# Decay blocks of 64 tokens instead of 128 in a chunked state-space scan, with the x of the states weighed from the transposed x

## What is computed

```python
x = layernorm(h); x = rmsnorm(x, norm_w)
z, xBC, dt_raw = split(x @ in_proj_w)          # 2048, 3072 and 32 columns
xs, B, C = split(silu(conv4(xBC) + conv_b))    # depthwise, 4 taps
dt = softplus(dt_raw + dt_bias); dA = exp(-dt * exp(A_log))
h_t = dA_t * h_{t-1} + (dt_t * x_t) B_t        # the scan over 512 tokens
y_t = h_t C_t + D * x_t
out = (groupnorm(y * silu(z)) * gate_norm_w) @ out_proj_w + residual
```

## Time and profile before

| | |
|---|---|
| median of 3 runs | 1308.03 us (1307.38 to 1315.56) |
| the profiled execution, its own time | 1308.41 us |
| its span in the trace | 1306.5 us |
| busy share: PE, DVE, ACT, POOL | 80%, 84%, 75%, 66% |
| instructions in the trace | 29881 |

### The profile page before, as it was taken

One profiled execution on the slowest core, in us unless ns is written; L12 is line 12 of the kernel. 1 busy time (PEld: TensorE's weight loads), 2 busy tenths in 40 slices (PEclk: granted clock), 3 DMA queues, 4 the chain that ended last, 5 costly groups with the idle time before them and its releaser, 6 DMA issues. The chain is left out here.

```text
span 1306.5 us, 29881 instructions
## 1 busy us (share of the span) xinstructions
PE 1042.0 (80%) x8556; PEld 718.9 (55%) x8556; DVE 1099.3 (84%) x1837; ACT 985.1 (75%) x2943; POOL 863.5 (66%) x584
## 2 busy tenths in 40 slices
PE   1423778888888888888888889979898888887786
PEld 1412555566555555665566566656566655653555
DVE  8756888889888888888888888888888999947995
ACT  3624778989788878888888888888888888862453
POOL 1540367877677868776777777776777888795321
PEclk9986789999899989998998998899988999998899
DMA  5532244534344334343443444443434344421301
GB/s 148 162 84 53 61 104 99 120 98 98 87 122 111 98 91 109 105 99 90 110 109 98 100 103 110 95 109 91 115 93 93 103 123 106 106 75 43 111 26 33
DMA packets 84864, 127.10 MB, mean 97 GB/s; under 512 B 18512, under 2 KB 29392, under 8 KB 84432
## 3 DMA queue, kind: packets, MB, share of 16 engines
q1 hardware_dynamic: 80464, 122.91, 37.4%
q10 hardware_dynamic: 4224, 2.10, 0.5%
HBM read 115.54 MB, written 9.44 MB: 96 GB/s over the span
## 5 line engine op out<-in xcount | busy, mean ns | idle before, releaser
L1047 DVE SCALAR_TENSOR_TENSOR conv<-bank,cw,conv 128x511 f32<-128x511 f32 (+2 forms) x576 | 412.0, 742 | 105.7 <-ACT conv L763 100.9
L619 POOL TENSOR_TENSOR lm<-lm,cbs 128x1024 f32<-128x1024 f32 x128 | 303.3, 2370 | 87.9 <-ACT xw L755 86.5
L1036 DVE TENSOR_TENSOR_SCAN lm<-spread,bank 128x512 f32<-128x512 f32 x256 | 297.5, 1203 | 16.5 <-issue 12.7
L796 ACT ACTIVATE xdt<-bank,dt_all 128x64 f32<-128x64 f32 x1024 | 221.0, 326 | 0.5 <-issue 0.5
L605 POOL TENSOR_TENSOR gated<-gated,gate 128x512 f32<-128x512 f32 x128 | 163.0, 1273 | 64.5 <-DVE gated L1079 62.7
L1347 PE MATMUL bank<-xn_hi,w_hi 128*128 (+1 forms) x320 | 161.1, 503 | 54.1 <-DVE conv L1047 54.1
L755 ACT ACTIVATE xw<-xdt,lm 128x64 f32<-128x64 f32 x768 | 196.2, 338 | 0.0
L625 POOL TENSOR_TENSOR ssum<-ssum,sq 128x512 f32<-128x512 f32 x96 | 123.5, 1287 | 109.8 <-ACT sq L810 107.5
L1408 PEld LDWEIGHTS bank<-lm,xdt 128*64 128x64 f32 x2048 | 112.6, 140 | 96.4 <-issue 95.6
L611 POOL TENSOR_TENSOR gated<-gated,rbs 128x512 f32<-128x512 f32 x128 | 164.1, 1283 | 1.5 <-ACT rbs L859 1.5
L763 ACT ACTIVATE conv<-bank,cb_bias,cw 128x512 f32<-128x512 f32 x192 | 142.2, 767 | 25.3 <-PE bank L1349 25.3
(11 more groups left out here) (167 smaller groups left out, 1676.3 us busy)
## 6 DMA issues: line engine op xcount, KB each, us to landing
spread<-decay_scratch SPq DMA_DIRECT2D x128, 512.0 KB, 5.1
spread<-product_scratch SPq DMA_DIRECT2D x256, 128.0 KB, 5.6
lm<-in_L_attn_in_proj_w SPq DMA_DIRECT2D x1, 2048.0 KB, 9.9
xn_scratch<-chan SPq DMA_DIRECT2D x4, 512.0 KB, 5.4
r_stage<-residual_scratch SPq DMA_DIRECT2D x8, 256.0 KB, 2.8
x_scratch<-r_stage SPq DMA_DIRECT2D x8, 256.0 KB, 5.6
cbs<-x_scratch SPq DMA_DIRECT2D x8, 256.0 KB, 3.0
gated<-x_scratch SPq DMA_DIRECT2D x1, 2048.0 KB, 8.2
```

The costliest lines, as they stand in the source:

```text
L619: gp.tensor_tensor(lm[:, mr, :, :], lm[:, mr, :, :], cbs[:, :, :], ALU.mult).then_inc(m_done, 1)
L796: act.activation(xdt[:, r, at:at + HP], misc_of("xt", n)[:, at:at + HP], ACT.Copy, scale=dt_h).then_inc(xdt_done, 1)
L1036: V.tensor_tensor_scan(lm[:, m % R, a, :], spread[:, m % R, a, :], ident_bank[:, :], 0.0, ALU.mult, ALU.add).then_inc(scanned, 1)
L1047: V.scalar_tensor_tensor(out=conv[:, ci % 4, shift:S], in0=tile_bank(b, n, t)[:, 0:S - shift], scalar=cw[:, q, t, KW - 1 - shift:KW - shif ...
```

## The change

The blocks become 64 tokens long, eight in a sequence instead of four.

- Two blocks now lie above each other in the partitions. DVE scans once 128x512 instead of twice; POOL multiplies by C B once 128x512 instead of 128x1024. `cdec` goes from DVE to POOL, and the copy of four block ends (`pend`, L743 on ACT) goes to POOL with eight.
- There are seven state steps instead of three on DVE, each 128x64, written between the taps one by one.
- PE makes seven states with 14 matmuls, eight of them (`s_low_done`) after the first half of the transposes of x and six after the second half. y takes 16 matmuls inside the blocks and 14 from the states, each of 64 columns and into quarters of two banks. C B takes 16 instead of 8 a unit.
- x for the states is no longer xdt times a column of lm. ACT weighs the transposed x itself in eight pieces by a table `wt_all` that is made in the set-up by masked sums (two matmuls for each of two masks) and exponentials. The products of decays come from the same sums, not from a scan on DVE.
- The two shared banks are gone. C B, bt, the norm factor and x for the next sequence go to the spare halves of the two y banks, and are copied by ACT in two halves of 256 columns each. For that ACT waits in each slot for `y_ready` of the slot.
- DVE's skip term is two operations of 4x64 columns and stands first in the next slot (lag 8) instead of last in the slot (lag 7).
- On PE the z tile stands between the two parts of y. On ACT silu now comes before the evacuation.

In the diff, cut to its core, `skip()` to `one_tap` is DVE's slot, the wait for `y_ready` stands on ACT between the square and the copies, and what follows it is the end of PE's slot.

```diff
+BLK = 64
+NBLK = S // BLK
...
-                    for a in range(2):
-                        V.tensor_tensor_scan(lm[:, m % R, a, :], spread[:, m % R, a, :], ident_bank[:, :], 0.0,
-                                             ALU.mult, ALU.add).then_inc(scanned, 1)
...
+                    V.tensor_tensor_scan(lm[:, m % (2 * R), :], spread[:, m % R, 0, :], seed_bank[:, :], 0.0,
+                                         ALU.mult, ALU.add).then_inc(scanned, 1)
...
-                    gp.tensor_tensor(lm[:, mr, :, :], lm[:, mr, :, :], cbs[:, :, :], ALU.mult).then_inc(m_done, 1)
...
+                    gp.tensor_tensor(lm[:, at, :], lm[:, at, :], cbs[:, v % 2, :], ALU.mult).then_inc(m_done, 1)
...
+                    gp.tensor_copy(pend[:, mr, :].unsqueeze(2),
+                                   spread[:, mr, 1, :].rearrange("p (k i) -> p k i", i=BLK)[:, :, BLK - 1:BLK]).then_inc(pend_done, 1)
...
+                    gp.tensor_tensor(cdec[:, mr, :], spread[:, mr, 1, :], chan[:, chan_of(v, 1), :], ALU.mult).then_inc(cdec_done, 1)
...
+                if yy is not None:
+                    skip()
+                if ssd is not None:
+                    scan()
+                work_list = []
+                if real:
+                    work_list += [(one_tap, (shift, t)) for shift in range(1, KW) for t in PLAN[r]]
+                for k in range(max(NBLK - 1, len(work_list))):
+                    if state is not None and k < NBLK - 1:
+                        state_step(k)
+                    if k < len(work_list):
+                        work_list[k][0](*work_list[k][1])
...
+                if back(b, n, LAG_Y) is not None:
+                    bb, m = back(b, n, LAG_Y)
+                    after(act, y_ready, SLOTS, bb, m)
...
+                    last.then_inc(y_intra_done, 1)
+                if ssd is not None:
+                    project(b, n, "z", ssd)
+                if yy is not None:
...
+                    for k in range(1, NBLK):
+                        c, e = divmod(k, 2)
...
+                            last = MM(y_bank[e][half, BLK * c:BLK * c + BLK], hpk[half, m % 2, k - 1, :],
+                                      cdec[half, m % R, BLK * k:BLK * k + BLK], start=False, stop=(k >= NBLK - 2))
```

More of the change, by code:

```diff
@@ L517, in _ @@
             store_rows(0)
[L518 removed]
+            sp.wait_ge(rows_stored[0], 48)
             for n in range(R):
@@ L1066, in decay_c @@
-                def decay_c():
-                    bb, m = ssd
-                    after(dve, c_copied, UNITS, bb, m // R)
-                    V.tensor_tensor(cdec[:, m % R, :], spread[:, m % R, 2, :], c_bank[:, :],
-                                    ALU.mult).then_inc(cdec_done, 1)
+                ssd, state, yy = (back(b, n, lag) for lag in (LAG_SSD, LAG_STATE, LAG_SUM))
                 def skip():
@@ L1366, in slot @@
                     after(pe, silu_done, NCONV, bb, CONV_ORDER.index((mq, 2 + mr)))
-                    misc_free(b, n, "xt")
-                    for c in range(CH):
-                        last = TR(misc_of("xt", n)[:, P * c:P * c + P], chan[:, chan_of(mq, 2 + mr), P * c:P * c + P], ident)
-                    last.then_inc(xt_ready, 1)
+                    xdt_there(pe, bb, m - 1)
+                    if r == 1 and back(b, n - 1, LAG_VAR) is not None:
+                        vb, vm = back(b, n - 1, LAG_VAR)
+                        after(pe, var_copied, UNITS, vb, vm // R)
+                    x_transposes(0)
+                if st is not None:
+                    states(0)
+                if ssd is not None:
+                    x_transposes(1)
+                else:
+                    if st is not None:
+                        after(pe, s_low_done, SLOTS, *st)
+                    out_projection()
+                if st is not None:
+                    states(1)
                 if real:
@@ new lines, in slot @@
+                if n == XN_SLOT and following(b) is not None:
+                    pe.wait_ge(staged, b * 16 + 16)
+                    for c in range(CH):
+                        last = TR(spare(c // 2)[:, P * (c % 2):P * (c % 2) + P], xn_stage[:, c, :], ident)
+                    last.then_inc(xnt_ready, 1)
+                if n == XO_SLOT and back(b, n, SLOTS) is not None:
+                    bb, _ = back(b, n, SLOTS)
+                    after(pe, out_copied, 1, bb, 0)
+                    for c in range(CH):
+                        last = TR(xo_half(b, c // 2)[:, P * (c % 2):P * (c % 2) + P], ocm[:, P * c:P * c + P], ident)
+                    last.then_inc(xo_ready, 1)
@@ L1463, in slot @@
-                if n == XO_SLOT and back(b, n, SLOTS) is not None:
-                    bb, _ = back(b, n, SLOTS)
-                    after(pe, out_copied, 1, bb, 0)
-                    misc_free(b, n, "xo")
-                    for c in range(CH):
-                        last = TR(misc_of("xo", n)[:, P * c:P * c + P], ocm[:, P * c:P * c + P], ident)
-                    last.then_inc(xo_ready, 1)
             def step(i, par, k):
```

639 lines of the change are left out of this document (309 added, 330 removed).

## The result

The changed kernel takes 1540.86 us (median of 4 runs, 1537.17 to 1544.68), the kernel before 1307.76 beside it: ratio 1.177, 95% interval 1.171 to 1.182. The forecast was 1425, in a range of 1330 to 1480. So the direction was right and the size was not: 233 us came where some 117 were expected.

The account below looks back on a forecast made before the run. A chain of waits (taps, z, y, ACT, next slot) was to bound the kernel: a unit of 35.3 plus branch 0.6 and clock 1.0, 36.9 against 32.9 us, +128 over 32 units, set-up -3: 1433, taken as 1425, range 1330 to 1480.

Parts of the forecast that it names:

- The mechanism: Loop: z waits for taps and y, and ACT with all behind it, waits for z; about 1425 us, chance 0.79.
- the same: Rival: slots r = 0 and r = 3 give back what r = 1 and 2 lose; 1295 to 1321 us, chance 0.05.
- PE is full: Rival: quarters don't pair, each small matmul runs alone, PE's slot grows from 7.25 to 10.8 us; about 1640, chance 0.03.
- the path into r = 2: First tap of r = 1 to that of r = 2: y_ready after 6.25 us, then ACT's way 3.65, sum 9.9.
- the path into r = 0: ACT must read x before PE transposes the next, 4.0 us, then PE's head 2.75: sum 6.8.
- The head of 2.7: PE's start of a slot to the evacuation: transposes, states, projection and shape changes take 2.7 us, bounds 2.15 and 3.1.
- Into r = 1: First tap of r = 0 to that of r = 1: PE's next slot waits for vtok, 8.9 us.
- the fifth tap ends at 4.2: DVE, slot r = 1: first tap to the end of the fifth, with two more state steps, takes 4.2 us.
- The clock, +1.0: PE's part of a unit's path, about 17 us, loses 1.0 us a unit to the low clock.
- The branch: Where the loop branches, once in four units, waiting adds 0.6 us a unit.
- Outside the slots: Set-up: spreads give back some 6 us, sums, exponentials and masked matmuls cost some 3; -3 in total.
- The faster rival: DVE's work decides: 0.6 to 0.9 us off each slot, 1195 to 1235 us, or 1265; chance 0.13.

Follow-up runs that it names:

- Experiments 1, 2 and 7: 1: changed kernel, taps tile by tile, 1438.52 us; 2: there z behind y, 1446.93; 7: kernel before, z between y's parts, 1392.26, with taps by tile 1317.86.
- reorderings of the same PE work: Changed kernel with taps tile by tile, first conv projection ahead of the state products, and ACT's gate ahead of its wait for y: 1313.64 us.
- Experiment 4: Changed kernel with ACT's gate ahead of its wait for y and of the copies: 1539.50 us.
- the head reordered in r = 2 alone: Changed kernel, in slots r = 2 only PE's first conv projection stands behind two transposes and ahead of the state products: 1488.12 us.
- a_head_r0: Changed kernel, in slots r = 0 only PE's first conv projection stands behind two transposes and ahead of the state products: 1501.77 us.
- the best order found here: Changed kernel with taps by tile, gate first, a tap ahead of each state step, and both conv projections ahead of the state products: 1266.63 us.
- two edits that gave 0 apart: On the 1314 us reordering of the changed kernel: tap ahead of each state step, 1316.06 us; both projections ahead of state products, 1318.66; together 1266.63.
- experiment 6: Changed kernel with taps by tile, z behind y, early projection and gate first (1322.20 us), without the weights-high by input-low product: 1329.36 us.
- the early head: Changed kernel with PE's first conv projection behind two transposes and ahead of the state products, in all four slots: 1410.48 us.

## Why the prediction was right in direction and short in size

- **The mechanism held.** z waits for the fifth tap, y for z, ACT's copies for y, and the next slot for the copies. Experiments 1, 2 and 7 show it from both kernels. The rivals fall with them: "the same", and "PE is full", since reorderings of the same PE work bring 227 us.
- **The step that failed: the path into r = 2, forecast 9.9, measured 11.3.** The forecast took ACT's way behind y as what binds: bt, gate, rexp, silus and evacuation, 3.65. Its price was about right, since in the turn shown ACT stood idle for 1.83 us ahead of the evacuation at 698.80, and so had made all of its way but the evacuation in 2.7. What binds is PE's head, which waits for the copies of B: 0.97 + 2.87 + 0.81 = 4.65 in the median turn, 1.0 more. The forecast named that wait only for DVE's skip, although it stands in the code of PE's slot. Experiment 4 confirms it: taking the gate's 0.6 us off ACT's way gives nothing. With the head reordered in r = 2 alone the stretch is 10.0, and 53 us come off. (The 8.7 that the forecast read for this stretch in the kernel before was one of the longer turns; its median is 8.2.)
- **The same kind of step: the path into r = 0, forecast 6.8, measured 7.5.** PE's head there waits for DVE's last state steps (four in a row, 1.22 us, each behind the one before). The forecast had counted the seven steps as work, and not asked who waits for the last. a_head_r0: 6.4, and 39 us. The two missed waits are 1.7 of the 3.1 us by which the unit was longer than forecast (40.0, not 36.9), some 54 of the 116 us between 1541 and 1425.
- **The head of 2.7** was 2.87 at the full clock, inside the bounds. Its parts were right: the eight pairs and a change take 0.61 start to start (0.63 forecast), the six 0.50 (0.51). In the turn shown it ran 3.55, its last products at 0.63 us each instead of 0.40, since the clock had fallen to 1.2 GHz; 7 of 26 heads at r = 2 had that.
- **"Into r = 1", 8.9, was 9.7, and this is the clock.** From PE's first transpose of r = 0 to that of r = 1 it is 8.7 (682.66 - 673.96, and the median), as forecast. But the head of r = 1 then takes 3.79 in the median, 0.9 more than the others, and 2.95 in the four units in which the clock was full there. Just before it PE makes the small matmuls of the sums of squares and waits for vtok (0.66 at 682.66). In the same stretch of low clock the slot's second projection takes longer, so ACT's second evacuation and the second tap come 0.34 late (688.95): **"the fifth tap ends at 4.2"** was 4.63, and 4.29 without that, so the price of the steps was right. From z to y_ready 1.97, forecast 2.05. "The clock, +1.0" spread a mean over PE's path. In the median unit the low clock costs some 1.2 in this one place, and more where it falls on other heads.
- **The branch** was forecast at 0.6 a unit. At each of the five branches inside the loop the stretch into r = 0 is 3.9 to 4.6 us longer than its median, 1.1 a unit. The other 0.5 between the sum of medians, 38.4, and the mean, 40.0, is slots that were slower than their median. That these 1.6 are as much as the forecast's 0.6 for the branch and 1.0 for the clock is luck: most of the clock's cost is in the medians. "Into r = 3" was close, 10.0 for 9.7.
- **Outside the slots** the forecast had -3. It is +3.2 ahead of the first tap and +13.6 behind the last. In the set-up the wait for the store fell by the 6 us forecast, to the 11.66 of the row below (was 17.84), so the rest of the set-up seems to have added more than the 3 forecast; which part of it isn't shown. Of the 13.6, 13.1 are there when the last matmul of the output projection starts (1201.9 before, 67.1 us behind the last tap; 1434.0 after, 80.2 behind). So they lie in the slots that empty the pipeline and not in the feed-forward layer; the forecast had no term for them.

```profile
100.38 0.59 ACT L747 ACTIVATE ssum<-bank 64x512 f32<-64x512 f32 x1 [11.66 <-DMA product_scratch<-ssum]
```

- **What was right:** DVE's work fell by 0.66 us a slot ((1099.3 - 1014.5) / 128; 0.6 to 0.9 forecast). POOL's cdec at 1.28, and the copy of eight columns at 0.20, the low end. The four quarters run together: 32 matmuls of y inside the blocks in 0.69, not 1.0. The Trainium skill ("TensorEngine Tiling (Array Packing)", The Solution) calls 64x64 tiles four independent ones; the trace agrees, with the 0.69.
- **The faster rival** (work decides, 1195 to 1265) had the potential nearly right: 1267 is what the same work takes in the best order found here. It was no forecast for this kernel, in which the order doesn't.

## What to carry to other kernels

When a product is moved ahead of another on an engine that works in order, list what each of the two waits for: here one product that waited for the fifth of six taps cost 83 us alone, and letting it go earlier gave 74 of them back, and moving it behind y in the changed kernel gave 94. List also every wait at the head of the slot, with its producer's place in its own queue; a producer that stands behind the moved work puts its delay ahead of everything. And if one reordering gives nothing, try it with its partner before dropping it: two edits that gave 0 apart gave 47 us together.

## What the runs showed of the hardware

- Leaving out ten matmuls a unit did not shorten the kernel: the granted clock fell from 0.97 to 0.93 over the same stretch (experiment 6). Shorter median slots and a lower clock cancelled.
- The clock depends on the order of work: 0.91 in the changed kernel and 0.97 with the early head, at PE busy shares of 81% and 83%.
- The low clock falls mostly on one place of the ring: 22 of 26 heads at r = 1 had it, 7 or 8 of 26 at the others.
- 32 matmuls of 64x64 tiles in four quarters take 0.69 us, 28 of y from the states, which use two quarters only, 1.03 (L1466).
